# Two key chunks in one maximum: b + relu(a - b), with Relu on ScalarE, and a group's operands loaded in six transfers

## The chip, the cores and the metric

One core of a Trainium2 chip. The number to predict is the device time of the whole kernel in microseconds, the median over runs.

## What is computed

Two transformer layers on 2048 tokens of width 128, each with adaptive layer norms, causal attention of 16 heads of width 8, and a mixture of experts. The change lies in the attention alone. For each layer:

```python
scores = jnp.einsum('bhqd,bhkd->bhqk', q, k) / jnp.sqrt(jnp.float32(HEAD_DIM))
scores = jnp.where(causal, scores, -jnp.inf)
attn = jax.nn.softmax(scores, axis=-1)
out = jnp.einsum('bhqk,bhkd->bhqd', attn, v)
```

Layer one has one sequence of 2048 tokens, with projections and rotary positions ahead of this; layer two runs through the same attention code with its own q and k.

## The kernel before, in words

**Operands.** Every float32 value of q and k is split into three bf16 parts (hi, mid, lo), stored in DRAM (`q_parts`, `k_parts`) and loaded as the nine products of parts: 9 x 8 rows of `QS` and `KS`, for the 4 heads of a group. Rows 96 to 103 of `QS` take the softmax's shift, so that the matmul of scores subtracts the row maximum by itself. Heads go in 4 groups of 4 (`GH`); two groups have buffers at a time (`QS[g % 2]`).

**Units and steps.** A unit is a pair (group g, query chunk Q of 512 tokens); `UNITS` lists 16 in a written order, numbered from 0. Unit 2 is (0, 2), unit 4 is (0, 3), unit 6 is (1, 3), unit 9 is (2, 3), and unit 10 is (3, 3), the first of group 3. A step is one block of 128 keys of a unit, 160 in a layer: scores of the four heads in two halves (TensorE, L931, with the causal mask at L935), Exp of each half (ScalarE, L978), and the product with the values (TensorE, L949).

**Maxima first.** Before a unit can be scored, the maximum of each query's scores must be known. For each head j, block qb of 128 queries and key chunk c of 512, TensorE makes a tile of scores in one of three rotating PSUM buffers (`mxb`, L898), 640 tiles a layer, and VectorE takes its maximum: a plain reduction (L996) below the diagonal, a masked add and maximum (L998) on it. When a unit's last tile is done, VectorE joins the chunks (L1003) and splits the result in two bf16 numbers; TensorE turns them into rows ("turn", L904), VectorE copies them (L1012), and SyncE moves the rows into `QS` (L838). Only then do the unit's scores run.

**Order.** `schedule()` (L77 to L159) writes one list, `ORDER`, in which tiles, turns, scores, values, and the normalization and output of finished units ("norm", "attT", "out") are interleaved. It keeps a clock for TensorE, VectorE and ScalarE by built-in costs and takes a tile when its buffer would be free before the next scores could start. A turn comes `TURN_LAG` tiles after its unit's last one. TensorE runs through this list strictly in order; so a wait in it holds everything behind it.

**Loads.** Group 0's rows are loaded by SyncE in pieces during the projections. Groups 1 to 3 are loaded by GpSimd's queue in `load_group` (L753): 13 transfers, of which 3 are under way. Group 1's start after the first shift row is in (`shift_set[0]`, L861), those of groups 2 and 3 after the last step of the group whose buffers they take (L870). SyncE's queue also issues the expert weights behind the turns (L841).

```python
for n, (dst, src) in enumerate(moves):
    if n >= UNDER_WAY:
        eng.wait_ge(done[n % UNDER_WAY], 16 * (before * PER_SEM[n % UNDER_WAY] + n // UNDER_WAY))
    eng.dma_start(dst, src).then_inc(done[n % UNDER_WAY], 16)
```

## Time and profile before

| | |
|---|---|
| median of 3 runs | 1350.62 us (1349.40 to 1352.48) |
| span of the profiled execution | 1351.6 us |
| TensorE busy | 1152.9 us, 85% |
| VectorE busy | 962.7 us, 71% |
| ScalarE busy | 695.5 us, 51% |
| GpSimd busy | 240.5 us, 18% |
| maximum tiles on TensorE (L898) | 5120 matmuls, 1280 tiles |
| plain maxima (L996) | 768 instructions, 497.3 us |
| masked maxima (L998) | 512 instructions, 240.9 us |
| Exp (L978) | 640 instructions, 545.1 us |

The span and the runs agree within 0.1%, and the profiled execution has no time of its own in the results beside its span. Attention takes some 62 to 527 us in layer one and 685 to 1150 us in layer two. Busy times of TensorE are long where matmuls overlap in its pipeline, so they say less than the starts do.

### The profile page before, as it was taken

The page shows a single profiled execution, that of the slowest core. Times are in us where ns is not written, and L with a number is a line of the kernel's source. Part 1 is how long each engine was busy: PE and PEld are TensorE (multiplying, and loading weights), DVE is VectorE, ACT ScalarE, POOL GpSimd, SP SyncE. Part 2 cuts the span into 40 slices and gives each one's busy share as a digit, 9 for nine tenths or more (in the row PEclk, how much of TensorE's full clock was granted, in tenths as well). Part 3 has the DMA queues.
Part 4 walks back from the last instruction along what each step waited for, and adds up shares of the span by engine and source line. Part 5 has one row for each costly group of instructions (what it writes and reads, how often), then busy time and mean ns, then how long its engine had stood idle before and what let it go on. Part 6 is the DMA issues. An engine that isn't in the chain of part 4 may idle for free. (4 is left out here: it accounts for less than half of the span.)

```text
span 1351.6 us, 39302 instructions
## 1 busy us (share of the span) xinstructions
PE 1152.9 (85%) x16626; PEld 581.8 (43%) x16627; DVE 962.7 (71%) x2700; ACT 695.5 (51%) x929; POOL 240.5 (18%) x271
## 2 busy tenths in 40 slices
PE   5878999999899997297368899999899999778993
PEld 4423434434344444175123343444334454546662
DVE  5888989989698853511558998989788882564553
ACT  4424657666567674142334465766666668323330
POOL 2440000101000000277121000100200000135761
PEclk9678989999899997599678898999999999689997
DMA  4441000503200000221353111330400000011123
GB/s 142 142 80 41 19 19 19 92 19 55 57 3 5 5 3 2 45 54 53 95 154 65 35 37 36 67 65 4 76 3 4 5 4 3 1 40 38 48 47 107
DMA packets 38022, 60.46 MB, mean 45 GB/s; under 512 B 6288, under 2 KB 29104, under 8 KB 36720
## 3 DMA queue, kind: packets, MB, share of 16 engines
q0 software_dynamic: 7648, 24.47, 9.2%
q1 hardware_dynamic: 30208, 33.57, 8.6%
q8 instruction: 129, 2.11, 0.7%
q14 instruction: 37, 0.30, 0.1%
HBM read 42.84 MB, written 14.12 MB: 42 GB/s over the span
## 5 line engine op out<-in xcount | busy, mean ns | idle before, releaser
L978 ACT ACTIVATE probs_at<-st 128x1024 f32<-128x1024 f32 (+3 forms) x640 | 545.1, 897 | 323.2 <-PE st L931 221.1
L996 DVE TENSOR_REDUCE mxp_at<-mx 128x1 f32<-128x512 f32 x768 | 497.3, 685 | 69.1 <-PE mx L898 67.6
L898 PE MATMUL mx<-ks,qs 128*32 128x512 bf16 (+3 forms) x5120 | 390.8, 367 | 40.5 <-DVE mxp_at L996 11.4
L931 PE MATMUL st<-qs,ks 128*32 128x512 bf16 (+3 forms) x5120 | 363.5, 355 | 10.6 <-DMA qs<-shrow_at 8.1
L949 PE MATMUL av<-probs_at,vs 128*32 128x512 f32 (+3 forms) x2560 | 290.9, 530 | 0.3
L898 PEld LDWEIGHTS mx<-ks,qs 128*32 128x32 bf16 x5120 | 137.2, 97 | 344.3 <-DVE mxp_at L996 140.6
L998 DVE CUSTOM_DVE_ANT_0 junk_at<-mx,maskN 128x384 f32<-128x384 f32 (+3 forms) x512 | 240.9, 485 | 39.3 <-PE mx L898 36.2
L931 PEld LDWEIGHTS st<-qs,ks 128*32 128x32 bf16 x5120 | 133.9, 98 | 97.8 <-ACT probs_at L978 22.6
L1274 POOL DMA_INDIRECT taken<-table,token x71 | 68.1, 959 | 251.1 <-DVEq L1063 218.3
L935 PE MATMUL st<-maskTb,identb 128*32 128x128 bf16 x2048 | 103.8, 220 | 0.0
L949 PEld LDWEIGHTS av<-probs_at,vs 128*32 128x32 f32 x2560 | 69.7, 111 | 47.8 <-issue 5.6
L768 POOL DMA_DIRECT2D qs<-in_zrow_dram x6 | 3.6, 598 | 404.0 <-PE av L949 390.1
L935 PEld LDWEIGHTS st<-maskTb,identb 128*32 128x32 bf16 x2048 | 55.4, 98 | 16.9 <-issue 1.9
L1612 DVE TENSOR_TENSOR hid_f<-st,sg_f 128x352 f32<-128x352 f32 x39 | 20.5, 525 | 49.4 <-ACT sg_f L1585 49.4
L1280 POOL DMA_INDIRECT eo<-eo_f,dest x39 | 38.4, 985 | 25.8 <-DVE eo_f L1623 22.5
L998 DVE DVE_READ_ACCUMULATOR2_ANT mxp_at<- 128x1 f32 x512 | 42.5, 83 | 0.0
L1585 ACT ACTIVATE sg_f<-st 128x352 f32<-128x352 f32 x39 | 18.1, 464 | 47.4 <-PE st L1531 47.4
L768 POOL DMA_DIRECT2D qs<-q_parts x54 | 28.0, 521 | 70.7 <-DMA qs<-q_parts 50.4
L1530 PE MATMUL st<-weights,hTt_f 128*128 x78 | 33.1, 507 | 8.5 <-ACT hTt_f L1579 5.8
L1361 POOL TENSOR_TENSOR weights<-weights,gates 128x384 f32<-128x384 f32 x1 | 1.0, 987 | 187.1 <-POOLq L823 187.1
L1579 ACT ACTIVATE hTt_f<-mx,modc 128x128 f32<-128x128 f32 x39 | 17.8, 458 | 27.2 <-PE mx L1525 27.1
L1531 PE MATMUL st<-weights,hTt_f 128*128 x78 | 29.4, 459 | 0.0
(271 smaller groups left out, 1043.5 us busy)
## 6 DMA issues: line engine op xcount, KB each, us to landing
qs<-q_parts POOLq DMA_DIRECT2D x54, 128.0 KB, 5.7
ks<-k_parts POOLq DMA_DIRECT2D x18, 384.0 KB, 6.7
weights<-in_w_dram SPq DMA_DIRECT2D x16, 256.0 KB, 3.0
table<-rows SPq DMA_DIRECT2D x8, 260.0 KB, 5.4
got_pj<-eo SPq DMA_DIRECT2D x4, 512.0 KB, 5.5
got_cb<-eo SPq DMA_DIRECT2D x4, 512.0 KB, 5.4
weights<-in_dw_dram SPq DMA_DIRECT2D x3, 576.0 KB, 4.9
weights<-in_gw_dram SPq DMA_DIRECT2D x3, 528.0 KB, 3.8
```

Of the source, the lines that this page charges most:

```text
L768: eng.dma_start(dst, src).then_inc(done[n % UNDER_WAY], 16)
L898: mm = pe.matmul(buf[z:z + 32, 0:w], QS[p][:, j, (4 * Q + qb) * P + z:(4 * Q + qb) * P + z + 32], KS[p][:, j, c * CH:c * CH + w], start=Tr ...
L931: mm = pe.matmul(st[half][z:z + 32, y, off:CH], KS[p][:, j, kb * P + z:kb * P + z + 32], QS[p][:, j, Q * CH + off:(Q + 1) * CH], start=Tru ...
L935: mm = pe.matmul(st[half][z:z + 32, y, off:off + P], m.identb[:, z:z + 32], m.maskTb[:], start=False, stop=True, tile_position=(0, z), ski ...
L949: mm = pe.matmul(avb[32 * j:32 * j + 32, off:CH], VS[p][:, kb, j, :], probs[:, s % 2, j, off:CH], start=kb == 0, stop=kb == TPC * Q + 3, t ...
L978: act.activation(probs[:, s % 2, 2 * half:2 * half + 2, off:CH], st[half][:, :, off:CH], ACT.Exp, scale=SCALE).then_inc(exp_done[half], 1)
L996: ins = v.tensor_reduce(dst, buf[:, 0:w], AX.X, ALU.max)
L998: ins = v.tensor_tensor_reduce(junk[:, k % MXBUF, 0:w], buf[:, 0:w], m.maskN[:, CH - w:], 1.0, -3e38, ALU.add, ALU.max, dst)
L1274: g.indirect_dma_start(out=m.got[e][:, t4], out_offset=None, in_=dram[f"table{L}"], in_offset=bass.IndirectOffsetOnAxis(ap=m.token[:, n:n ...
L1280: g.indirect_dma_start(out=dram[f"eo{L}"], out_offset=bass.IndirectOffsetOnAxis(ap=m.dest[:, n:n + 1], axis=0), in_=rows, in_offset=None). ...
L1530: pe.matmul(G[z % 2][:, 0:FF1], hT[z % 2][:], gw[:, bass.ds(e, 1), :], start=True, stop=True)
L1531: pe.matmul(U[z % 2][:, 0:FF1], hT[z % 2][:], uw[:, bass.ds(e, 1), :], start=True, stop=True).then_inc(gu_ready, 1)
```

## The change

For units with Q of 2 or 3 the tile of key chunk 0 (a) and its reduction go. In its place TensorE makes a tile of the difference, q times (k0 - k1), a matmul with the same queries against a new operand `KD`; ScalarE writes relu of it to one of three SBUF buffers; and VectorE, when the tile of chunk 1 (b) is there, adds and takes the maximum in one two-input instruction: max(a, b) = b + relu(a - b). `KD` is made once per layer by GpSimd from the stored parts of k (nine instructions of 128x512, one behind the other), stored to DRAM, and loaded like k, with a copy per group buffer. SyncE waits for that store (`kd_stored`) before its first shift row. The planner's costs change, and it knows the new tiles; `UNITS`, the order of units, stays. The 13 transfers of a group become six that are issued without a wait between them: zero rows, k, three of q, and `KD`. Group 1's load waits for the shift of unit 1 (`shift_set[1]`).

```diff
 def max_tiles(g, Q):
-    return [(g, Q, j, qb, c) for qb in range(TPC) for j in range(GH) for c in range(Q + 1)]
+    return [(g, Q, j, qb, c) for qb in range(TPC) for j in range(GH) for c in range(Q >= 2, Q + 1)]
+
+
+def paired(m):
+    return m[1] >= 2 and m[4] == 1
 
 
...
+def max_order():
+
+    tiles = [m for g, Q in UNITS for m in max_tiles(g, Q)]
+    at = [i for i, m in enumerate(tiles) if paired(m)]
+    ahead = {}
+    for i in at:
+        ahead.setdefault(max(0, i - DIFF_LEAD), []).append(tiles[i])
+    out, due = [], []
+    for i, m in enumerate(tiles):
+        out += [("diff", x) for x in ahead.get(i, [])]
+        out.append(("max", m))
+        if due and due[0][0] <= i:
+            out.append(("turn", due.pop(0)[1]))
+        u = UNITS.index(m[:2])
+        if i + 1 == len(tiles) or UNITS.index(tiles[i + 1][:2]) != u:
+            due.append((i + TURN_LAG, u))
+    return out + [("turn", u) for _, u in due]
...
-LOADS = 1 + Q_LOADS + K_LOADS
-UNDER_WAY = 3
-PER_SEM = [len(range(z, LOADS, UNDER_WAY)) for z in range(UNDER_WAY)]
+LOADS = 1 + 1 + 3 + 1
...
-def load_group(eng, m, L, dram, g, done, before):
-
-
-    q, k = (dram[f"{n}_parts{L}"].tensor for n in "qk")
-    moves = [(m.QS[g % 2][SHIFT0:SHIFT0 + 2 * GH], bass.AP(dram["zrow"].tensor, 0, [[T, 2 * GH], [0, GH], [1, T]]))]
+def load_diff(eng, m, L, dram, g, done):
+
+    eng.dma_start(m.KD[g % 2][0:9 * HD].rearrange("p j t -> p (j t)"), bass.AP(
+        dram[f"kd_parts{L}"].tensor, g * GH * CH, [[0, 3], [H * CH, 3 * HD], [1, GH * CH]])).then_inc(done, 16)
+
+
+def load_group(eng, m, L, dram, g, done):
+
+    clear_shift(eng, m, dram, g % 2, done)
+    eng.dma_start(m.KS[g % 2][0:9 * HD].rearrange("p j t -> p (j t)"), bass.AP(
+        dram[f"k_parts{L}"].tensor, g * GH * T, [[0, 3], [H * T, 3 * HD], [1, GH * T]])).then_inc(done, 16)
     for a in range(3):
-        for b in range(3):
-            r = (3 * a + b) * HD
-            moves.append((m.QS[g % 2][r:r + HD], bass.AP(q, (a * P + g * GH) * T, [[H * T, HD], [T, GH], [1, T]])))
-    for a in range(3):
-        r = 3 * a * HD
-        moves.append((m.KS[g % 2][r:r + 3 * HD], bass.AP(k, g * GH * T, [[H * T, 3 * HD], [T, GH], [1, T]])))
-    for n, (dst, src) in enumerate(moves):
-        if n >= UNDER_WAY:
-            eng.wait_ge(done[n % UNDER_WAY], 16 * (before * PER_SEM[n % UNDER_WAY] + n // UNDER_WAY))
-        eng.dma_start(dst, src).then_inc(done[n % UNDER_WAY], 16)
+        eng.dma_start(m.QS[g % 2][3 * a * HD:3 * (a + 1) * HD].rearrange("p j t -> p (j t)"), bass.AP(
+            dram[f"q_parts{L}"].tensor, (a * P + g * GH) * T, [[0, 3], [H * T, HD], [1, GH * T]])).then_inc(done, 16)
+    load_diff(eng, m, L, dram, g, done)
...
                 loads = list(weight_loads)
+                sp.wait_ge(kd_stored, 16 * (L + 1))
                 for item in ORDER:
...
+                hi, mid, lo = (m.parts[1][:, a, :] for a in range(3))
+                d, t = (m.weights[:, KD_AT + i * CH:KD_AT + (i + 1) * CH] for i in range(2))
+                kd = m.weights[:, KD_AT + 2 * CH:KD_AT + 2 * CH + 3 * CH // 2].bitcast(BF).rearrange("p (a c) -> p a c", a=3)
+
+                def chained(ins):
+                    ins.then_inc(kd_chain.sem, 1)
+                    g.wait_ge(kd_chain.sem, kd_chain.next())
+
+                chained(g.tensor_tensor(d, hi[:, 0:CH], hi[:, CH:2 * CH], ALU.subtract))
+                chained(g.tensor_tensor(t, mid[:, 0:CH], mid[:, CH:2 * CH], ALU.subtract))
+                chained(g.tensor_tensor(d, d, t, ALU.add))
+                chained(g.tensor_tensor(t, lo[:, 0:CH], lo[:, CH:2 * CH], ALU.subtract))
+                chained(g.tensor_tensor(d, d, t, ALU.add))
+                chained(g.tensor_copy(kd[:, 0], d))
+                chained(g.tensor_tensor(t, d, kd[:, 0], ALU.subtract))
+                chained(g.tensor_copy(kd[:, 1], t))
+                chained(g.tensor_tensor(kd[:, 2], t, kd[:, 1], ALU.subtract))
+                g.dma_start(bass.AP(dram[f"kd_parts{L}"].tensor, 0, [[CH, P], [P * CH, 3], [1, CH]]), kd).then_inc(kd_stored, 16)
+                for p in range(2):
+                    g.memset(m.KD[p][64:P].bitcast(F32), 0.).then_inc(kd_set, 1)
+                g.wait_ge(kd_set, 2 * (L + 1))
+                g.wait_ge(kd_stored, 16 * (L + 1))
+                load_diff(g, m, L, dram, 0, kd_first)
                 if L == 0:
                     for z, rows in enumerate((KS[1], QS[1])):
                         g.memset(rows[64:P].bitcast(F32), 0.).then_inc(pool_set, 1)
                         g.wait_ge(pool_set, 5 + z)
                     g.dma_start(KS[1][SHIFT0:SHIFT0 + 2 * GH], dram["zo"]).then_inc(s_("ones_in1"), 16)
-                g.wait_ge(shift_set[0], 16 * (L * (NU // 4) + 1))
-                load_group(g, m, L, dram, 1, kq_loaded[1], loads_before(1))
+                g.wait_ge(shift_set[1], 16 * (L * (NU // 4) + 1))
+                load_group(g, m, L, dram, 1, kq_loaded[1])
...
-                    pe.wait_ge(mx_free, RB + k + 1)
-                    if kind == "max":
+                    if k >= MXBUF and ROT[k - MXBUF][0] == "diff":
+                        pe.wait_ge(diff_done, L * ND + DIFF_OF[ROT[k - MXBUF][1]] + 1)
+                    else:
+                        pe.wait_ge(mx_free, freed(k - MXBUF) if k >= MXBUF else MXBUF + L * NDVE)
+                    if kind in ("max", "diff"):
                         gg, Q, j, qb, c = x
...
+                        if kind == "diff" and k == DIFFS[0]:
+                            pe.wait_ge(kd_first, 16 * (L + 1))
+                        keys = m.KD[p][:, j, :] if kind == "diff" else KS[p][:, j, c * CH:c * CH + w]
                         for z in range(0, P, 32):
                             mm = pe.matmul(buf[z:z + 32, 0:w], QS[p][:, j, (4 * Q + qb) * P + z:(4 * Q + qb) * P + z + 32],
-                                           KS[p][:, j, c * CH:c * CH + w], start=True, stop=True, tile_position=(0, z), skip_group_check=True)
+                                           keys, start=True, stop=True, tile_position=(0, z), skip_group_check=True)
                         mm.then_inc(mx_ready, 1)
                     elif kind == "turn":
                         pe.wait_ge(shift_split, UB + x + 1)
...
-                for s, (g, Q, kb) in enumerate(STEPS):
-                    off = step_off(s)
-                    act.wait_ge(av_done, SB + s + 1)
-                    for half in range(2):
+                def rectify(k):
+                    n = DIFF_OF[ROT[k][1]]
+                    if n >= RELUS:
+                        act.wait_ge(mx_free, freed(ROT_OF[ROT[DIFFS[n - RELUS]][1]]))
+                    elif L:
+                        act.wait_ge(mx_free, MXBUF + NDVE)
+                    act.wait_ge(mx_ready, RB + k + 1)
+                    act.activation(relu[:, n % RELUS], mxb[k % MXBUF][:], ACT.Relu).then_inc(diff_done, 1)
+
+                for item in ORDER:
+                    if item[0] == "rot" and ROT[item[1]][0] == "diff":
+                        rectify(item[1])
+                    elif item[0] == "scores":
+                        _, s, half = item
+                        off = step_off(s)
+                        if half == 0:
+                            act.wait_ge(av_done, SB + s + 1)
                         act.wait_ge(st_ready[half], SB + s + 1)
                         act.activation(probs[:, s % 2, 2 * half:2 * half + 2, off:CH], st[half][:, :, off:CH], ACT.Exp,
                                        scale=SCALE).then_inc(exp_done[half], 1)
-                    if kb == 0 and s:
-                        evacuate(UNIT[s] - 1)
+                        if half == 1 and STEPS[s][2] == 0 and s:
+                            evacuate(UNIT[s] - 1)
                 evacuate(NU - 1)
...
                     v.sem_inc(mx_free, MXBUF)
                 for k, (kind, x) in enumerate(ROT):
+                    if kind == "diff":
+                        continue
                     buf = mxb[k % MXBUF]
                     v.wait_ge(mx_ready, RB + k + 1)
                     if kind == "max":
                         g, Q, j, qb, c = x
                         u, w = UNITS.index((g, Q)), max_width(x)
                         dst = mxp[:, u % 4, qb * GH + j, c:c + 1]
-                        if c < Q:
+                        if paired(x):
+                            n = DIFF_OF[x]
+                            v.wait_ge(diff_done, L * ND + n + 1)
+                            ins = v.tensor_tensor_reduce(relu[:, n % RELUS], buf[:], relu[:, n % RELUS], 1.0, -3e38, ALU.add, ALU.max, dst)
+                        elif c < Q:
                             ins = v.tensor_reduce(dst, buf[:, 0:w], AX.X, ALU.max)
                         else:
                             ins = v.tensor_tensor_reduce(junk[:, k % MXBUF, 0:w], buf[:, 0:w], m.maskN[:, CH - w:], 1.0, -3e38,
                                                          ALU.add, ALU.max, dst)
                         ins.then_inc(mx_free, 1)
                         if (j, qb, c) == (GH - 1, TPC - 1, Q):
-                            v.wait_ge(mx_free, RB + k + 1 + MXBUF)
-                            v.tensor_reduce(mx[:, u % 4, :], mxp[:, u % 4, :, 0:Q + 1], AX.X, ALU.max, negate=True).then_inc(max_final, 1)
+                            v.wait_ge(mx_free, freed(k))
+                            v.tensor_reduce(mx[:, u % 4, :], mxp[:, u % 4, :, Q >= 2:Q + 1], AX.X, ALU.max, negate=True).then_inc(max_final, 1)
```

Here `NDVE` counts the rotating tiles that VectorE frees and `freed(k)` those up to tile k; `DIFF_OF` numbers the difference tiles.

Three places of the new order, each as it was and as it is.

SyncE at the start of layer one's attention (`stored1`, `stored2` say that the parts of k are in DRAM; `shrow_at` is the row of shifts):

```order
L748 DMA ks<-k_parts 24x4x512 [waits stored1]
L748 DMA ks<-k_parts 24x4x512 x2
L748 DMA ks<-k_parts 24x4x1024 [waits stored2]
L748 DMA ks<-k_parts 24x4x1024 x2
L838 DMA qs<-shrow_at 8x4x512 [waits shift_row] x3
L842 DMA weights<-in_w_dram 128x512 x2
```

```order
L794 DMA ks<-k_parts 24x4x512 [waits stored1]
L794 DMA ks<-k_parts 24x4x512 x2
L794 DMA ks<-k_parts 24x4x1024 [waits stored2]
L794 DMA ks<-k_parts 24x4x1024 x2
L892 DMA qs<-shrow_at 8x4x512 [waits shift_row,kd_stored]
L892 DMA qs<-shrow_at 8x4x512 [waits shift_row] x2
L896 DMA weights<-in_w_dram 128x512 x2
L892 DMA qs<-shrow_at 8x4x512 [waits shift_row]
```

The first shift row has a second condition, `kd_stored`, and all later ones stand behind it.

TensorE around the turn of unit 2 in layer one: the last steps of unit 1, then tiles, the turn (`nsh_at`), and tiles up to the scores of unit 2. In the count of a row four matmuls are one tile:

```order
L931 MATMUL st<-qs,ks 32x128 x4
L935 MATMUL st<-maskTb,identb 32x128 x4
L949 MATMUL av<-probs_at,vs 32x256 x4
L898 MATMUL mx<-ks,qs 32x512 x36
L898 MATMUL mx<-ks,qs 32x128 x4
L898 MATMUL mx<-ks,qs 32x512 x4
L904 MATMUL mx<-identb,nsh_at 8x128 x4
L898 MATMUL mx<-ks,qs 32x128 x4
L898 MATMUL mx<-ks,qs 32x512 x4
L898 MATMUL mx<-ks,qs 32x128 x4
L898 MATMUL mx<-ks,qs 32x512 x4
L898 MATMUL mx<-ks,qs 32x128 x4
```

```order
L1019 MATMUL st<-qs,ks 32x128 x4
L1023 MATMUL st<-maskTb,identb 32x128 x4
L1037 MATMUL av<-probs_at,vs 32x256 x4
L986 MATMUL mx<-ks,qs 32x512 x4
L986 MATMUL mx<-ks,qs 32x128 x4
L986 MATMUL mx<-ks,qs 32x512 x4
L992 MATMUL mx<-identb,nsh_at 8x128 x4
L986 MATMUL mx<-ks,qs 32x128 x4
L986 MATMUL mx<-ks,qs 32x512 x4
L986 MATMUL mx<-ks,qs 32x128 x4
L986 MATMUL mx<-ks,qs 32x512 x4
L986 MATMUL mx<-ks,qs 32x128 x4
```

Between the last values of unit 1 and the turn stood 11 tiles; now 3 do, and all of unit 2's other tiles stand ahead of that.

ScalarE at the start of unit 6's scores in layer one (the copy moves the finished sums of unit 5):

```order
L978 ACTIVATE probs_at<-st 128x2x128 [waits st_ready1]
L978 ACTIVATE probs_at<-st 128x1024 [waits st_ready0,av_done]
L978 ACTIVATE probs_at<-st 128x1024 [waits st_ready1]
L971 COPY avs_at<-av 128x512 [waits mx_ready,av_done]
L978 ACTIVATE probs_at<-st 128x1024 [waits st_ready0,av_done]
L978 ACTIVATE probs_at<-st 128x1024 [waits st_ready1]
L978 ACTIVATE probs_at<-st 128x1024 [waits st_ready0,av_done]
```

```order
L1068 ACTIVATE relu_at<-mx 128x512 [waits mx_ready,mx_free]
L1079 ACTIVATE probs_at<-st 128x1024 [waits st_ready0,av_done]
L1068 ACTIVATE relu_at<-mx 128x512 [waits mx_ready,mx_free]
L1079 ACTIVATE probs_at<-st 128x1024 [waits st_ready1]
L1059 COPY avs_at<-av 128x512 [waits mx_ready,av_done]
L1068 ACTIVATE relu_at<-mx 128x512 [waits mx_ready,mx_free]
L1079 ACTIVATE probs_at<-st 128x1024 [waits st_ready0,av_done]
L1079 ACTIVATE probs_at<-st 128x1024 [waits st_ready1]
L1068 ACTIVATE relu_at<-mx 128x512 [waits mx_ready,mx_free]
L1079 ACTIVATE probs_at<-st 128x1024 [waits st_ready0,av_done]
L1079 ACTIVATE probs_at<-st 128x1024 [waits st_ready1]
```

Relus stand between Exps, some between the two halves of one step.

## Rows read from the trace of the kernel before

**Rows 1.** Busy time by stretch: us, then each engine's (instructions), clock, DMA share, GB/s
```profile
62.00:77.50 15.50, 9.89 (x116) 3.29 (x120) 14.83 (x50) 0.00 (x0) 8.41 (x5) 0.61 0.49 129
...
191.00:344.00 153.00, 150.75 (x2688) 65.21 (x2684) 135.58 (x340) 105.75 (x123) 14.73 (x28) 0.99 0.25 49
...
354.00:495.00 141.00, 139.08 (x2604) 63.87 (x2604) 118.84 (x345) 96.49 (x118) 0.00 (x0) 0.99 0.03 7
```

**Rows 2.** Timeline of ScalarE, layer one: start, us, what, [idle before, releaser]
```profile
98.85 1.02 ACT L978 ACTIVATE probs_at<-st 128x1024 f32<-128x1024 f32 x1 [10.94 <-PE st L931]
...
131.17 2.16 ACT L978 ACTIVATE probs_at<-st 128x1024 f32<-128x1024 f32 x2 [12.40 <-PE st L931]
...
192.13 1.02 ACT L978 ACTIVATE probs_at<-st 128x1024 f32<-128x1024 f32 x1 [10.60 <-PE st L931]
...
356.12 1.94 ACT L978 ACTIVATE probs_at<-st 128x1024 f32<-128x1024 f32 x2 [11.03 <-PE st L931]
```

**Rows 3.** Load of group 3: timeline of GpSimd and TensorE; DMA issues, KB, us to landing
```profile
319.54 0.58 POOL L768 DMA_DIRECT2D qs<-in_zrow_dram  x1 [61.79 <-PE av L949]
...
349.11 0.83 PE L898 MATMUL mx<-ks,qs 128*32 128x512 bf16 x12 [4.12 <-DMA ks<-k_parts]
...
qs<-q_parts POOLq DMA_DIRECT2D x54, 128.0 KB, 5.7
ks<-k_parts POOLq DMA_DIRECT2D x18, 384.0 KB, 6.7
```

**Rows 4.** Timeline of TensorE in a long stretch
```profile
404.81 1.03 PE L949 MATMUL av<-probs_at,vs 128*32 128x512 f32 x8
...
405.67 0.77 PE L898 MATMUL mx<-ks,qs 128*32 128x384 bf16 x12
...
406.26 0.60 PE L931 MATMUL st<-qs,ks 128*32 128x512 bf16 x8
...
406.69 0.39 PE L898 MATMUL mx<-ks,qs 128*32 128x512 bf16 x4
```

**Rows 5.** Groups by line and shape, TensorE, 361 to 495 us: busy, mean ns
```profile
L931 PE MATMUL st<-qs,ks 128*32 128x512 bf16 x588 | 44.9, 379 | 0.0
...
L898 PE MATMUL mx<-ks,qs 128*32 128x512 bf16 x488 | 40.7, 381 | 0.5 <-DVE mxp_at L998 0.2
...
L949 PE MATMUL av<-probs_at,vs 128*32 128x512 f32 x296 | 38.2, 592 | 0.0
```

**Rows 6.** Timeline and groups of VectorE and ScalarE, 131 to 344 us
```profile
241.35 1.88 DVE L996 TENSOR_REDUCE mxp_at<-mx 128x1 f32<-128x512 f32 x3
...
L998 DVE CUSTOM_DVE_ANT_0 junk_at<-mx,maskN 128x512 f32<-128x512 f32 x28 | 19.0, 687 | 3.1 <-PE mx L898 3.1
...
L971 ACT COPY avs_at<-av 128x512 f32<-128x512 f32 x7 | 4.1, 585 | 0.0
```

**Rows 7.** The starts of both attentions: timelines; GpSimd's groups; DMA issues
```profile
68.42 0.61 POOL L850 COPY vs<-vall 128x512 f32<-128x512 f32 x1 [9.99 <-DMA k_parts<-weights]
...
74.59 52.78 SPq L838 DMA_DIRECT2D qs<-shrow_at  x3
...
77.53 0.65 PE L931 MATMUL st<-qs,ks 128*32 128x512 bf16 x4
...
691.49 0.61 POOL L850 COPY vs<-vall 128x512 f32<-128x512 f32 x1 [5.53 <-DMA k_parts<-weights]
...
705.09 0.62 PE L931 MATMUL st<-qs,ks 128*32 128x512 bf16 x4 [3.96 <-DMA qs<-shrow_at]
...
L503 POOL TENSOR_TENSOR weights<-res,weights 128x512 bf16<-128x512 f32 x8 | 9.9, 1246 | 7.2 <-ACT weights L348 7.2
...
L220 POOL TENSOR_TENSOR qf<-tmp 128x512 f32<-128x512 f32 x4 | 6.2, 1552 | 25.3 <-DVE tmp L400 25.3
...
k_parts<-weights SPq DMA_DIRECT2D x4, 384.0 KB, 3.7
```

**Rows 8.** Waits, 150 to 500 us: waiting, releaser, us in total, times, longest
```profile
PEld st L931 <- ACT probs_at L978: 3.4, 10, 0.6
```

126 lines of the change are left out of this document (80 added, 46 removed).

## The prediction

> **What bounds the kernel now.** First the busy table by stretches of the first layer's attention [rows 1]. It shows two kinds of stretch. In the long ones (191 to 344, 354 to 495 us, and 131 to 181 like them) TensorE is busy 150.8 of 153 and 139.1 of 141 us, VectorE 89% and 84%, ScalarE 69% and 68%. In short ones like 344 to 354 us ScalarE is all but idle: no unit of scores is ready.
>
> The timeline of ScalarE gives these holes their length [rows 2]: it waits for scores 10.94, 12.40, 10.60 and 11.03 us, at the starts of units 1, 2, 4 and 9. Layer two repeats all four. The first three are VectorE's: a unit can't be scored before all its maxima are taken. The fourth is not: TensorE waits 4.12 us for keys of the next group [rows 3], and the turn of unit 9 stands three tiles behind that wait.
>
> Is a "busy" TensorE full? Its matmul ends are modelled, so I go by starts [rows 4]: from 406.26 to 406.69 eight score matmuls take 0.43 us, eight value matmuls 0.86 (404.81 to 405.67), three maximum tiles 0.59 (405.67 to 406.26), so a 512-wide one about 0.21. With these, the counts of 361 to 495 us [rows 5] make: 588 wide score matmuls 31.6 us, 488 of maxima 26, 296 of values 31.6; masks, narrow forms and transposes, in proportion to their width, about 33. That is 122 us of work in 134. The other 12 us, 9%, are gaps, most of them ahead of maximum tiles whose buffer VectorE still holds. So TensorE bounds the long stretches with VectorE close behind, and what VectorE gives up there is worth only TensorE's small gaps.
>
> **The change, part by part.** (a) Units with Q of 2 or 3 give up one reduction per head and block: 8 units x 16 = 128 a layer. One costs VectorE 0.60 us: three in a row take 1.88, of which the last 0.68 [rows 6]. The pass that stays becomes the two-input form. The masked pass, which also reads PSUM and SBUF, takes 687 ns at this width, as long as a reduction, so the exchange adds nothing. VectorE loses 128 x 0.60 = 77 us a layer. TensorE's tiles stay 640 a layer, since each pair has a difference tile in place of chunk 0's. ScalarE gains 128 Relus. Nearest row: the copy of the same width from PSUM, mean 585 ns [rows 6]. Two Exps of 1.02 us take 1.94 together [rows 2], so some 0.10 overlap and a Relu costs 0.48: 61 us a layer. 64 of them fall into 191 to 344 us, where ScalarE goes from 105.8 to 137 of 153 us, with little slack.
>
> (b) **The long stretches**, 344 us a layer. A share of 9% would be 31 us. Turns, transposes and some scores hold part of it, and a difference tile will now wait for ScalarE, behind Exps of 1.02 us. I take 9 us a layer as gained, between 0 and 31: -18.
>
> (c) **The hole before unit 2.** Before, 11 tiles stand between the last scores of unit 1 and the turn of unit 2; now 3 do (order rows of TensorE). Eight at 0.60 us are 4.8, less 0.8 for what was packed ahead of it, part of that into the hole before unit 1, which is otherwise the same: -4 a layer, -8. Behind the turn stand 10 tiles where 9 did, and its row's way through VectorE, SyncE and the DMA stays. The hole before unit 4 has 9 tiles ahead of its turn before and after, and 11 instead of 7 behind it: I put it at 0, between -3 and +2.
>
> (d) **The load of a group.** Thirteen transfers, three under way, run from 319.54 to 349.11 us, 29.6 us [rows 3]; keys come last. Six issue at once, in some 3 us. The 384 KB pieces land in 6.7 us with three under way, 176 GB/s; the 128 KB ones in 5.7, 69 GB/s. The new load carries 2.8 MB (zero rows, q, k, and 0.3 for the difference): 16 us at the first rate, 20 with issue and landing. It is there at 340, before TensorE asks at 345, and the 10 us hole shrinks to 7 tiles and the turn's way, 3.2 us: -7 a layer, -14. At the old length it gives nothing. Group 1 now waits for the shift of unit 1 instead of unit 0: its load would run from 107 to 127 us, just before TensorE wants it at about 128 (the end of unit 1's scores, 118.5, plus the delay of (e)). What is late there is lost; I price it at 0.
>
> (e) **The start.** This is the cost. GpSimd now does 9 steps of 128x512 behind the copy that ends at 69.03 us, and SyncE holds the first shift row until their store has landed. Seven subtractions or additions at 1.2 us (the 1246 ns row) and two casts at 0.9 (between that and the copy's 0.61), with handshakes 0.5: 10.7 us. The store is like the 384 KB one: 3.7, plus issue 0.5. So the row leaves at 83.9 instead of 74.59, and with the 2.94 us that it takes until TensorE starts at 77.53, the first scores come at 86.9: +9.3 [rows 7]. In layer two the copy ends at 692.10, so they come at 709.9 instead of 705.09: +4.8. Nothing hides it: TensorE stands in front of the first scores, VectorE starves behind it, and unit 1's maxima shift too. The granted clock at the start is 0.61 [rows 1], the lower of two levels for much of it, and a longer idle time should keep it low: +2 for both. Together +16. Bounds: 9 steps at 0.61 and at 1.55 us (GpSimd's slowest two-input row) give +4 and +28. The zeroing of the second buffers, 3.5 us each, comes behind all this, but before group 1's load asks for GpSimd.
>
> Sum: +16 - 18 - 8 + 0 - 14 = **-24 us** against the profiled span of 1351.6: 1327.6. The median of the runs is 1.0 lower: **1327**.
>
> A rule speaks against (a): the Trainium skill, ScalarE: Activation LUTs, Rules for kernel authors, sends relu to VectorE, and budgets about 0.3 us plus 0.83 ns an element for an ACTIVATE. By that estimate a Relu is 0.73 us, ScalarE would be busy 152 of the 153 us, term (b) would be gone and the sum would give 1345. The copy's row has 0.585 before any overlap, so the sum goes by the row.
>
> **Rivals.** *ScalarE's queue becomes the wait* (slower). ScalarE works in order: a Relu often stands behind an Exp of 1.02 us, and until it is done one of only three rotating buffers is held; the Exps behind it move back by 0.48 us and the next scores with them. For it: ScalarE at 89%, and Relus between the two Exps of a step in the new order. Against: tiles and scores are interleaved anew with the Relus in their place, and scores hardly wait for Exps now, 3.4 us in 350 [rows 8]. If one Relu in four costs TensorE half an Exp, 64 x 0.51 = 33 us, (b) turns from -18 to +33 and the sum is +27: 1378. It decides from +6 in (b), 0.02 us lost per Relu.
>
> *The loads gain nothing and the start costs nearly its upper bound* (no change). Six transfers share the same DMA engines; if the small pieces' 69 GB/s is what they get, (d) is 0 and the sum is -10; with the start at +26 it is 0: 1351.
>
> *VectorE was the pace after all* (faster still). If three quarters of the 9% go, (b) is -46 and the sum -52: 1299. Against: it needs a ScalarE that is never late.
>
> That the change doesn't do what it says can be excluded for the maxima, whose instructions the order shows; for the load it is the second rival.
>
> **Chances.** Forecast (1303 to 1347) 0.56; the larger gain 0.12; no change 0.07; slower, by ScalarE's queue or by a start at its upper bound with late loads, 0.25. A measurement of this kernel tells 0.2% (2.7 us) from no change: faster 0.68, same 0.07, slower 0.25. The range, **1302 to 1361**, leaves out about 1 in 10 on each side and holds the bounds of (e) with those of (d), and half the way to the first rival.
>
> **What would show it.** VectorE's busy time falls by about 150 us and ScalarE's rises by 120 to 150. The idle time before unit 2 falls from 12.4 to about 8 us, that before unit 9 from 11 to about 4. The first scores come at 87 us, in layer two 5 us later than before by the end of its projections. In the long stretches gaps ahead of maximum tiles become rare, and new waits for a Relu stay at a few us. Wrong would be: ScalarE over 90% busy there with TensorE waiting for it, keys that still arrive 25 us after their trigger, or first scores later than 92 us.

## The result and the profile after

The changed kernel takes **1401.57 us** (median of 4 runs, 1399.91 to 1403.02) where the kernel before, run beside it, took 1351.55: a ratio of 1.0363, 95% interval 1.0330 to 1.0395. It is slower by 50 us; the forecast was 24 us faster, and its range ended at 1361. The profiled execution has a span of 1398.1 us, 46.5 more than before.

Busy times first, from the page's first and fifth part (busy time, mean ns, idle time before it and what ended it):

```profile
PE 1162.2 (83%) x16626; PEld 589.6 (42%) x16627; DVE 817.3 (58%) x2700; ACT 827.2 (59%) x1185; POOL 247.1 (18%) x255
...
L1079 ACT ACTIVATE probs_at<-st 128x1024 f32<-128x1024 f32 (+3 forms) x640 | 557.5, 900 | 147.3 <-PE st L1019 78.7
...
L1105 DVE CUSTOM_DVE_ANT_0 junk_at<-mx,maskN 128x384 f32<-128x384 f32 (+3 forms) x512 | 241.6, 485 | 72.9 <-PE mx L986 69.8
L1101 DVE CUSTOM_DVE_ANT_0 relu_at<-mx,relu_at 128x512 f32<-128x512 f32 x256 | 176.9, 691 | 181.3 <-PE mx L986 178.9
...
L1068 ACT ACTIVATE relu_at<-mx 128x512 f32<-128x512 f32 x256 | 154.1, 602 | 82.1 <-PE mx L986 77.8
L1103 DVE TENSOR_REDUCE mxp_at<-mx 128x1 f32<-128x512 f32 x256 | 175.9, 687 | 28.9 <-PE mx L986 28.6
...
L986 PE MATMUL mx<-kd_at,qs 128*32 128x512 bf16 x1024 | 107.5, 398 | 32.4 <-DMA kd_at<-kd_parts 29.1
```

VectorE gives up 145 us and ScalarE takes on 132, as intended. What is new stands in the last row: TensorE waits 29.1 us for the differences' keys, which did not exist before. An order that puts other work there could have hidden them.

The three stretches of [rows 1], at their new places (columns as there):

```profile
62.00:82.40 20.40, 9.35 (x96) 2.74 (x92) 12.73 (x47) 0.00 (x0) 14.95 (x15) 0.58 0.31 90
206.00:354.00 148.00, 139.55 (x2386) 59.29 (x2381) 92.84 (x307) 121.07 (x164) 8.14 (x14) 0.98 0.25 49
380.00:518.00 138.00, 136.08 (x2552) 61.63 (x2552) 98.98 (x335) 109.16 (x145) 0.00 (x0) 1.00 0.02 4
```

VectorE falls from 89% to 63% of the second stretch, and it was to be TensorE's gain; but TensorE is busy 139.6 of 148 us there where it was busy 150.8 of 153. ScalarE is at 82% there; 89% was forecast.

Where are the 46.5 us? ScalarE copies the value sums once at each unit's start. Those copies date the units in both traces (start of the copy, us):

| unit | 1 | 4 | 5 | 6 | 9 | 12 | 13 | end of 15 |
|---|---|---|---|---|---|---|---|---|
| before, layer one | 101.1 | 194.4 | 235.5 | 267.0 | 357.9 | 461.2 | 480.7 | 520.1 |
| after | 107.1 | 200.9 | 244.6 | 285.8 | 380.7 | 481.6 | 504.3 | 543.4 |
| before, layer two | 729.7 | 822.4 | 863.5 | 895.7 | 984.9 | 1089.6 | 1109.0 | 1148.4 |
| after | 757.2 | 851.2 | 895.0 | 937.4 | 1033.1 | 1134.0 | 1156.7 | 1195.8 |

The loss by stretch is 6.0 up to unit 1, then 17.3 in the attention of layer one (436.3 against 419.0 us), 4.2 up to unit 1 of layer two, 19.9 in its attention (438.6 against 418.7), and 0.9 gained behind it: 46.5. In both layers nearly all of it falls between units 4 and 6 (12.3 and 12.9), between 6 and 9 (3.8 and 6.6) and between 12 and 13 (3.3 in both). From unit 9 to 12, the longest stretch without a load, the new kernel is faster, by 2.4 and 3.8 us. The 4.2 us are less sure than the rest: among the versions below that share one start, the time from the end of one attention to unit 1 of the next goes from 208.5 to 214.5 us.

The load of group 2, as [rows 3] had that of group 3, in the timeline of GpSimd and TensorE:

```profile
243.95 0.57 POOL L774 DMA_DIRECT2D qs<-in_zrow_dram  x1 [135.78 <-PE av L1037]
244.51 0.63 POOL L808 DMA_DIRECT2D ks<-k_parts  x1
...
246.95 0.62 POOL L801 DMA_DIRECT2D kd_at<-kd_parts  x1
...
259.80 0.61 PE L1019 MATMUL st<-qs,ks 128*32 128x512 bf16 x2 [3.50 <-issue]
...
273.78 0.62 PE L986 MATMUL mx<-kd_at,qs 128*32 128x512 bf16 x4 [2.66 <-DMA kd_at<-kd_parts]
```

The DMA issues of the page, with the KB of one and the us from issue to landing:

```profile
ks<-k_parts POOLq DMA_DIRECT2D x6, 1152.0 KB, 3.9
qs<-q_parts POOLq DMA_DIRECT2D x18, 384.0 KB, 16.1
...
kd_at<-kd_parts POOLq DMA_DIRECT2D x8, 288.0 KB, 24.9
```

All six are issued within 3.6 us, yet TensorE can go on only 29.8 us after the trigger. Group 3's load takes 27.2: triggered at 339.20, used at 366.42.

The landing times of the first two rows can't be taken singly. All six transfers add to one semaphore, and the profile tells a landing by its count. Between 243.9 and 248.5 us, when the keys' 1152 KB would have landed, the load's queue moved 0.40 MB in all (packets, MB, share of 16 engines' time):

```profile
q0 software_dynamic: 635, 0.40, 52.2%
```

Near its end the load is thin. Only a fifth of the DMA engines' time is taken, at 83 GB/s (columns as in [rows 1]):

```profile
263.00:268.00 5.00, 5.00 (x94) 2.44 (x90) 3.12 (x17) 3.73 (x4) 0.00 (x0) 0.99 0.21 83
```

Group 3's wait, and the hole before unit 2, are what ScalarE's timeline still shows of [rows 2]:

```profile
136.52 2.01 ACT L1079 ACTIVATE probs_at<-st 128x1024 f32<-128x1024 f32 x2 [10.32 <-PE st L1019]
...
367.15 0.60 ACT L1068 ACTIVATE relu_at<-mx 128x512 f32<-128x512 f32 x1 [9.53 <-PE mx L986]
```

The start, answering to [rows 7]:

```profile
65.37 0.61 POOL L904 COPY vs<-vall 128x512 f32<-128x512 f32 x1 [8.47 <-DMA k_parts<-weights]
66.06 1.16 POOL L919 TENSOR_TENSOR weights<-weights 128x512 f32<-128x512 bf16 x1
...
74.37 0.61 POOL L926 CAST weights<-weights 128x512 bf16<-128x512 f32 x1
75.06 1.15 POOL L927 TENSOR_TENSOR weights<-weights 128x512 bf16<-128x512 f32 x1
...
79.71 0.85 SPq L892 DMA_DIRECT2D qs<-shrow_at  x1
...
82.41 0.62 PE L1019 MATMUL st<-qs,ks 128*32 128x512 bf16 x4 [8.27 <-DMA qs<-shrow_at]
```

And the waits of 150 to 500 us, answering to [rows 8], which had 3.4 us for Exps (waiting, releaser, us in total, times, longest). First two rows of the kernel before, then the changed kernel:

```profile
PEld mx L898 <- DVE mxp_at L996: 54.1, 165, 0.7
PEld mx L898 <- DVE mxp_at L998: 34.0, 117, 0.5
```

```profile
PEld mx L986 <- DVE mxp_at L1105: 26.5, 91, 0.5
PEld mx L986 <- DVE mxp_at L1101: 25.3, 65, 1.2
...
PEld mx L986 <- ACT relu_at L1068: 14.9, 42, 0.7
PEld mx L986 <- DVE mxp_at L1103: 13.5, 42, 0.8
...
PEld st L1019 <- ACT probs_at L1079: 11.0, 27, 0.8
```

The weight loads of maximum tiles waited 88.1 us for VectorE before and wait 65.3 now. But 14.9 us for Relus are new, and the waits for Exps have grown from 3.4 to 11.0: most of what VectorE gives up is waited for elsewhere. These waits partly overlap with matmuls that still run, so they aren't lost time one for one.

### The profile page after: what moved, and what is told of

Its sections match the earlier page's. It is cut to its first block and busy times, and to the rows that moved or that the text cites. A ratio compares the mean times of both kernels' runs of the same rounds, so it can differ in the third digit from the quotient of the medians.

```text
span 1398.1 us, 40050 instructions
## 1 busy us (share of the span) xinstructions
PE 1162.2 (83%) x16626; PEld 589.6 (42%) x16627; DVE 817.3 (58%) x2700; ACT 827.2 (59%) x1185; POOL 247.1 (18%) x255
## 5 line engine op out<-in xcount | busy, mean ns | idle before, releaser
L1079 ACT ACTIVATE probs_at<-st 128x1024 f32<-128x1024 f32 (+3 forms) x640 | 557.5, 900 | 147.3 <-PE st L1019 78.7
L986 PE MATMUL mx<-ks,qs 128*32 128x512 bf16 (+3 forms) x4096 | 325.0, 361 | 35.3 <-DVE mxp_at L1101 9.0
L1037 PE MATMUL av<-probs_at,vs 128*32 128x512 f32 (+3 forms) x2560 | 295.4, 535 | 0.3
L1101 DVE CUSTOM_DVE_ANT_0 relu_at<-mx,relu_at 128x512 f32<-128x512 f32 x256 | 176.9, 691 | 181.3 <-PE mx L986 178.9
L986 PEld LDWEIGHTS mx<-ks,qs 128*32 128x32 bf16 x4096 | 113.7, 98 | 271.4 <-DVE mxp_at L1105 73.8
L1068 ACT ACTIVATE relu_at<-mx 128x512 f32<-128x512 f32 x256 | 154.1, 602 | 82.1 <-PE mx L986 77.8
L1103 DVE TENSOR_REDUCE mxp_at<-mx 128x1 f32<-128x512 f32 x256 | 175.9, 687 | 28.9 <-PE mx L986 28.6
L986 PE MATMUL mx<-kd_at,qs 128*32 128x512 bf16 x1024 | 107.5, 398 | 32.4 <-DMA kd_at<-kd_parts 29.1
L986 PEld LDWEIGHTS mx<-kd_at,qs 128*32 128x32 bf16 x1024 | 29.2, 96 | 86.8 <-issue 38.6
L1637 PE MATMUL st<-weights,hTt_f 128*128 x78 | 33.0, 505 | 8.8 <-ACT hTt_f L1686 5.9
```

The lines of the kernel that those rows point to most:

```text
L986: mm = pe.matmul(buf[z:z + 32, 0:w], QS[p][:, j, (4 * Q + qb) * P + z:(4 * Q + qb) * P + z + 32], keys, start=True, stop=True, tile_positi ...
L1037: mm = pe.matmul(avb[32 * j:32 * j + 32, off:CH], VS[p][:, kb, j, :], probs[:, s % 2, j, off:CH], start=kb == 0, stop=kb == TPC * Q + 3, t ...
L1068: act.activation(relu[:, n % RELUS], mxb[k % MXBUF][:], ACT.Relu).then_inc(diff_done, 1)
L1079: act.activation(probs[:, s % 2, 2 * half:2 * half + 2, off:CH], st[half][:, :, off:CH], ACT.Exp, scale=SCALE).then_inc(exp_done[half], 1)
L1101: ins = v.tensor_tensor_reduce(relu[:, n % RELUS], buf[:], relu[:, n % RELUS], 1.0, -3e38, ALU.add, ALU.max, dst)
L1103: ins = v.tensor_reduce(dst, buf[:, 0:w], AX.X, ALU.max)
```

## The experiments

Five causes were on the table: the length and order of the group loads, the time at which the order asks for them, the start, ScalarE's queue, and the planner's other numbers. Ratios are to the kernel before, with 95% intervals. The kernel before was run anew beside each group of experiments, with medians of 1353.3 to 1356.0 us; so between groups ratios tell more than microseconds.

**The five transfers alone**, in the kernel before (no difference, no pairing, old order):

```diff
-LOADS = 1 + Q_LOADS + K_LOADS
-UNDER_WAY = 3
-PER_SEM = [len(range(z, LOADS, UNDER_WAY)) for z in range(UNDER_WAY)]
+LOADS = 1 + 1 + 3
...
-    for n, (dst, src) in enumerate(moves):
-        if n >= UNDER_WAY:
-            eng.wait_ge(done[n % UNDER_WAY], 16 * (before * PER_SEM[n % UNDER_WAY] + n // UNDER_WAY))
-        eng.dma_start(dst, src).then_inc(done[n % UNDER_WAY], 16)
```

> The kernel before with its loads of groups 1 to 3 in five transfers issued without waits (zero rows, k, three of q); everything else as before, no difference operand. Theory A (the unthrottled load is the fault: it fills the DMA engines, is no quicker in all, and delays TensorE's instruction fetch): the keys arrive about 24 to 28 us after the trigger instead of 29, waits of 2 to 4 us with no releaser appear on TensorE during the loads, three to five of them, and the time is 1350 to 1360. Theory B (Relus in ScalarE's queue are the fault and the loads are fine): the waits of 4.1 and 2.5 us for keys go with the holes around them, no new waits, 1335 to 1343. I expect A: 1353.

1355.98 us, ratio 1.0015 (0.9990 to 1.0040): no change. The wait for keys at group 3 is gone (unit 9's copy at 355.6 instead of 357.9), but group 1's load now runs beside the turn and shift row of unit 1: TensorE stands 6.03 us at 89.77 us, in the middle of a run of mask matmuls and with no releaser, 15.8 us behind that load's trigger, and in layer two it waits 5.15 us for unit 1's row instead of 1.88. Three to five such stalls were expected; there is one. The transfers as such neither give nor take in sum.

**The start.** SyncE's wait for the differences' store goes from ahead of the first shift row to ahead of the first expert weights.

```diff
-                sp.wait_ge(kd_stored, 16 * (L + 1))
                 for item in ORDER:
...
+                            if u == 2:
+                                sp.wait_ge(kd_stored, 16 * (L + 1))
```

> The changed kernel with SyncE's wait for the store of the difference moved from ahead of the first shift row to ahead of the first expert weights, whose region it protects. The first scores should come about 5 us earlier in layer one and 3 to 4 in layer two (the row then waits for VectorE alone). Theory C (the start is lost one for one, since TensorE stands behind it): 1392 to 1394 against 1401.6. Theory D (the start is hidden by a later wait, for the difference operand of group 1 or for its load): no change within 2 us. I expect C: 1393.

1393.77 us, ratio 1.0303 (1.0257 to 1.0350): 8 us of the 50. The copy of unit 1 comes at 97.6 us instead of 107.1; the attentions are 3.3 us longer and 0.9 shorter (439.6 and 437.7). The start's cost was the wait, not GpSimd's work.

**Fourteen transfers, three under way**, in the changed kernel (an excerpt; pieces of 8 and 24 rows as before, the difference's keys second):

```diff
+        if n >= UNDER_WAY:
+            eng.wait_ge(done[n % UNDER_WAY], 16 * (before * PER_SEM[n % UNDER_WAY] + n // UNDER_WAY))
```

> The changed kernel with its loads of groups 1 to 3 as before: pieces of 8 and 24 rows, three under way, the difference operand as one more transfer, the second of 14. Same order of tiles as the changed kernel. Theory A: the 12 us of waits without a releaser vanish, but the load takes 29 to 31 us, so that the 31 us of waits at the first tiles of groups 2 and 3 stay or grow by a few us, since the order asks for them early: 1390 to 1402. Theory B: nothing changes but the loads' own length: 1400 to 1410.

1435.56 us, ratio 1.0612 (1.0563 to 1.0660), 34 us slower still, and above what was expected. Three waits of TensorE in layer one alone:

```profile
135.76 1.15 PE L998 MATMUL mx<-ks,qs 128*32 128x512 bf16 x12 [11.63 <-DMA ks<-k_parts]
...
287.53 0.62 PE L998 MATMUL mx<-kd_at,qs 128*32 128x512 bf16 x4 [14.27 <-DMA ks<-k_parts]
...
388.56 0.62 PE L998 MATMUL mx<-kd_at,qs 128*32 128x512 bf16 x4 [16.85 <-DMA ks<-k_parts]
```

With this order every group is waited for: the six first tiles of groups wait 85.9 us in all, where they waited 34.3 with six transfers at once. Groups 2 and 3 of layer one take 36.1 and 34.6 us from trigger to first tile instead of 29.8 and 27.2. So the same bytes come sooner as six transfers. The 34 us are less than the 51.6 us of added waits: some of those waits took the place of others. TensorE's stalls without a releaser in mid-stream (3.50, 3.17 and 1.80 us in the changed kernel) are gone here, as the expectation had it; the kernel before has none either.

**Unpaired, all else kept** (`paired` returns False, chunk 0 gets its tile again):

> The changed kernel with the maxima as before: no difference tiles, no Relu, plain reductions for chunks 0 and 1; the difference operand is still made, stored and loaded, and the planner keeps the new costs, with its order made for these tiles. It tells what the pairing itself is worth beside loads and start. Theory B: the Relus cost some 30 us, so this gains: 1365 to 1375. Theory A: the pairing gives nothing and costs nothing in the long stretches but makes the order ask for groups 2 and 3 earlier (9 steps after the trigger instead of 13), so part of the waits for loads goes: 1378 to 1390. Theory E (the pairing gains what was forecast in the holes and long stretches, 10 to 20 us a layer, and other things hide it): 1405 to 1425.

1378.73 us, ratio 1.0185 (1.0143 to 1.0227): 23 us less. Taking the pairing out of this kernel gains. And no keys are waited for at groups 2 and 3: with unpaired tiles the planner asks for group 2 in step 60, with paired ones in step 56. Stalls without a releaser remain, of 2.34, 2.22 and 4.16 us, each 18 to 19 us behind the trigger of a load.

**The planner's numbers alone**: the unpaired version without any difference (no steps on GpSimd, no store, five transfers):

> The changed kernel with no difference of keys at all: unpaired maxima, five transfers a group, nothing computed or waited for at the start, group 1 asked after unit 0's shift as before. What is left of the change is the planner's new costs, and thereby the order of the units, beside the five transfers at once (which alone made 1356.0). Theory A (the order and the loads cost the rest): the unpaired version with the difference kept took 1378.7; less 8 for the start, 1368 to 1373. Rival (the numbers of the planner are harmless, and the unpaired version lost its time by the start and by the difference's own transfers): 1353 to 1360.

1358.06 us, ratio 1.0020 (0.9997 to 1.0044). The new costs do no harm without pairing (attention of layer one 415.4 us, before 419.0). The 1368 to 1373 that my theory gave was a miss; the rival's range held it. Against the unpaired version with the difference, the attentions are 8.3 and 9.0 us shorter. Beside the start, it differs by the difference's own transfer and by asking for group 1 a unit earlier, so the transfer of 288 KB may cost much of that; it wasn't taken apart.

**The load reckoned at 28 us** in the changed kernel:

```diff
-LOAD_US = 18.
+LOAD_US = 28.
```

> The changed kernel with one number of its planner raised: a group's load is reckoned 28 us instead of 18, so the order takes the first tile of group 2 in step 60 instead of 56 and that of group 3 in step 91 instead of 88; the transfers are the same. Theory A (the waits for the difference's keys, 30.8 us in four places, are lost outright): 1401.6 - 20 to 30 = 1372 to 1382. Theory B (VectorE and ScalarE fall behind elsewhere, the wait for keys only takes the place of another): 1392 to 1402.

1380.94 us, ratio 1.0212 (1.0173 to 1.0252): 21 us for one number. The waits for the differences' keys shrink from 30.8 us to 1.7, 1.2 and 2.9, all in layer two. A stall without a releaser stays, in the middle of eight score matmuls, 15.6 us behind a trigger. First TensorE's timeline, then the instruction queue's packets of 226 to 241 us, of 242 to 257.5 and of 258 to 260.2 (there none is listed):

```profile
260.14 0.39 PE L1019 MATMUL st<-qs,ks 128*32 128x512 bf16 x2 [3.23 <-issue]
```

```profile
q8 instruction: 3, 0.05, 1.4%
...
q8 instruction: 1, 0.02, 0.6%
```

From 226 to 241 us, ahead of the trigger at 244.57, three packets of instructions came in; in the 15.5 us with the load, one. That fits a TensorE that has run out of instructions while the queues are full. Such stalls stand in the versions with five or six transfers at once and in none with three under way; that it is the instructions wasn't tested apart, so it stays a reading.

**The same, with the difference asked for early and the store's wait late.** The difference of a group goes out when the last difference tile two groups back is done, on its own semaphore; that of group 1 goes out at the start (an excerpt):

```diff
+                    g.wait_ge(diff_done, L * ND + LAST_DIFF[gg - 2] + 1)
+                    load_diff(g, m, L, dram, gg, kd_in[gg % 2])
                     g.wait_ge(av_done, 2 + SB + LAST[gg - 2] + 1)
```

> As with the planner's 28, and the difference's keys of a group asked for as soon as the last difference tile two groups back is done, on a semaphore of their own, so that five transfers are left for the trigger; and SyncE's wait for the store of the difference moved from ahead of the first shift row to ahead of the first expert weights. Theory A with the start: 8 less than the version with 28 alone for the start and 2 to 6 less for the shorter load: 1360 to 1372. Theory B (ScalarE's queue costs it): no lower than 1385.

1365.53 us, ratio 1.0079 (1.0046 to 1.0112). 8 of the 15 us are the start, by the run above. Layer one's attention is down from 424.8 to 419.4 us; layer two's is up from 426.2 to 430.2. There the early difference of group 3 falls into group 2's load, 11 us behind the trigger, and TensorE waits at the first tile of group 2, which waits for that load:

```profile
866.53 0.56 POOL L776 DMA_DIRECT2D qs<-in_zrow_dram  x1 [55.73 <-PE av L1045]
...
877.45 0.62 POOL L803 DMA_DIRECT2D kd_at<-kd_parts  x1 [7.48 <-ACT relu_at L1076]
...
899.20 0.62 PE L994 MATMUL mx<-kd_at,qs 128*32 128x512 bf16 x4 [5.74 <-issue]
```

**The planner's old costs** in the changed kernel (handshakes, pace, Exp, row's way, 26 us for a load; the Relu's cost kept):

```diff
-CLOCK = 2330.
-LOAD_US = 18.
+CLOCK = 2400.
+LOAD_US = 26.
-    to_dve = to_act = .23
-    back = .13
+    to_dve = to_act = .2
+    back = .1
-            act = max(act, pe + to_act, av_end.get(s - 2, 0) + back) + .07 + 2 * w * .000833
+            act = max(act, pe + to_act) + .19 + 2 * w * .000833
```

(also 45 us instead of 55 for group 1, 2.4 instead of 2.8 for the row, 0.003 a matmul instead of 0.012)

> The changed kernel, pairing, six transfers and start kept, with the planner's costs and latencies put back to those of the kernel before (load 26 us, shorter handshakes, Exp with 0.19 fixed), the Relu's cost kept. The first tile of group 2 comes in step 58, that of group 3 in step 90. Theory A: the waits for keys fall by half or more, 1380 to 1390. Rival (the new numbers describe the chip better and the old ones would make a worse order): 1400 or more.

1372.10 us, ratio 1.0135 (1.0104 to 1.0166), 29 us less with start and loads as in the change, and less than either theory gave.

**q asked for only when the keys have landed**, on the 1365.5 version:

```diff
+    eng.wait_ge(done, 16 * (LOADS * before + 2))
     for a in range(3):
```

> The version with the plan at 28, the difference's keys early and the store's wait late (1365.5), with one thing more: GpSimd waits until the zero rows and the keys of a group have landed before it asks for the three transfers of q, so 1.2 and then 1.2 MB are under way instead of 2.4. Theory A2 (a full set of DMA queues holds back TensorE's instruction fetch: waits of 5.7 and 2.8 us with no releaser in layer two): those waits shrink and the time is 3 to 8 us lower, 1357 to 1362. Rival (the load only gets longer, as with three small transfers under way): 1368 or more, with new waits for q.

1398.73 us, ratio 1.0330 (1.0297 to 1.0364), 33 us slower. The rival was right. First TensorE at the first tiles of groups 1 and 2, then what this run alone shows of the load: the landings, the keys now apart from q, and a window in which all but one packet are the keys' (columns as in [rows 1]):

```profile
127.52 1.15 PE L995 MATMUL mx<-ks,qs 128*32 128x512 bf16 x12 [10.36 <-issue]
...
276.64 0.62 PE L995 MATMUL mx<-kd_at,qs 128*32 128x512 bf16 x4 [7.94 <-issue]
```

```profile
ks<-k_parts POOLq DMA_DIRECT2D x6, 1152.0 KB, 17.7
qs<-q_parts POOLq DMA_DIRECT2D x18, 384.0 KB, 9.6
```

```profile
247.00:259.00 12.00, 12.00 (x192) 4.57 (x184) 9.08 (x30) 10.48 (x13) 0.00 (x0) 1.00 0.20 83
```

The keys alone take 17.7 us, not 3.9, and leave four fifths of the DMA engines' time unused: 83 GB/s at a share of 0.20, the pace of the end of the load in the changed kernel. Three of 16 engines would be a share of 0.19, and the source of the keys starts with a dimension of three copies (`[[0, 3], ...]` in `load_group`), as do those of q and of the difference. Whether another form of these transfers would be faster wasn't tried. With q held back behind the keys, the two can't overlap, and group 2's load takes 34.9 us, though the difference's keys aren't in it.

The two waits of TensorE shown above are at first tiles of a group, where it waits for the load. So "issue" at a group's first tile is the load, and I had read the 5.74 us above wrongly as instructions when I wrote this expectation. The stall in mid-group at 260.14 is another thing.

**A shorter Relu**, 64 of 512 columns, in the 1365.5 version (it leaves out part of the maximum; the other columns hold a constant, and VectorE writes its sum elsewhere):

```diff
-                    act.activation(relu[:, n % RELUS], mxb[k % MXBUF][:], ACT.Relu)
+                    act.activation(relu[:, n % RELUS, 0:64], mxb[k % MXBUF][:, 0:64], ACT.Relu)
```

> The 1365.5 version with a Relu over 64 of the 512 columns; the other columns of its output hold a constant, and VectorE still adds and reduces 512, so the maximum that is subtracted is too large (it leaves out part of the maximum and its output is not the reference's). VectorE's second operand no longer overwrites the Relu's buffer. Theory B (ScalarE's queue: Relus hold back Exps and tiles): a Relu costs some 0.25 us less, 32 us a layer off ScalarE, and half to all of the 4 us a layer that pairing costs against the unpaired order, and of the 9 that it should have brought, comes: 1340 to 1357. Rival (TensorE is full and nothing that the other two engines give up is worth anything): 1361 to 1367.

1355.54 us, ratio 0.9997 (0.9974 to 1.0019), 10 us less, in theory B's range. A Relu takes 227 ns instead of 602 (groups of 150 to 500 us):

```profile
L1077 ACT ACTIVATE relu_at<-mx 128x64 f32<-128x64 f32 x108 | 24.5, 227 | 28.7 <-PE mx L995 25.1 <-DVE mxp_at L1116 2.9
```

96 us off ScalarE's work (256 x 0.375) give 10. But of these, 1.8 and 7.8 us come from the two attentions, most of the latter at group 3 of layer two; the long stretches give under 1 us each.

**Old costs, early difference, late store wait** together:

> The 1365.5 version with the old costs in the planner (as the 1372 version has them). That one lost 8 us at the start and some 2 us by loads; both are mended here: 1360 to 1364. Theory A says that the two mends add up, 1360; if the order is what the early keys make useless, 1365 to 1368.

**1347.62 us, ratio 0.9936 (0.9913 to 0.9960)**: 0.6% faster than the kernel before, clear of noise, and 12 us below the expectation. The early difference of group 3 now goes out 18.6 us behind the trigger:

```profile
855.47 0.56 POOL L776 DMA_DIRECT2D qs<-in_zrow_dram  x1 [52.44 <-PE av L1045]
...
874.07 0.62 POOL L803 DMA_DIRECT2D kd_at<-kd_parts  x1 [15.15 <-ACT relu_at L1076]
```

and at a group's first tile TensorE waits 1.0 us at most (group 1 of layer two). The attentions take 415.3 and 414.4 us.

**The unpaired version with group 1's load behind unit 1's row** (new costs, no difference):

```diff
-                g.wait_ge(shift_set[0], 16 * (L * (NU // 4) + 1))
+                g.wait_ge(shift_set[1], 16 * (L * (NU // 4) + 1))
```

> The unpaired order with the new planner costs and five transfers at once (1358.1), with group 1's load asked for after the shift row of unit 1 instead of unit 0. There TensorE waited 4.96 us for instructions at 91.2 and 4.18 us for the row of unit 1 at 733.0, both beside that load; without them 1348 to 1352, the first version below the kernel before. Rival (group 1's load is then late by what the row gains): 1355 to 1360.

1352.19 us, ratio 0.9992 (0.9958 to 1.0026): by the medians 6 us less than with the load ahead of the row, by the ratios 4, with intervals that overlap. The copy of unit 1 comes at 98.1 instead of 105.1 us.

**Which of the old numbers?** Four runs on the 1365.5 version. The Exp's cost alone:

> The 1365.5 version (plan at 28, early difference, late store wait, new planner costs) with the Exp's old cost alone (0.19 us fixed instead of 0.07, and not tied to the values two steps back). If it is this number that made the order with pairing 18 us slower than the old costs do (1347.6), 1348 to 1356; if it is the handshakes, 1362 to 1370.

1372.56 us, ratio 1.0109 (1.0074 to 1.0145), above both expectations. The handshakes and the pace alone:

> The 1365.5 version with the old handshakes and TensorE pace alone (0.20 and 0.10 us instead of 0.23 and 0.13, 0.003 a matmul instead of 0.012, 2.4 GHz instead of 2.33). The counterpart of the run with the old Exp cost: 1348 to 1356 if the handshakes were it, 1362 to 1370 if the Exp's cost was.

1369.99 us, 1.0096 (1.0065 to 1.0128). The row's way and group 1's time:

> The 1365.5 version with the two old numbers that neither of the last two runs put back: the turn row's way 2.4 us instead of 2.8 and group 1's load in at 45 instead of 55. If these carry the 18 us, 1347 to 1354; if the old costs only work together, 1363 to 1372.

1366.38 us, 1.0082 (1.0048 to 1.0116). And the first two together:

> The complement: old Exp cost and old handshakes together, the row's way 2.8, group 1 at 55 and the load at 28 as in the 1365.5 version. Its first tile of group 2 comes in step 58 and its tiles before the trigger of group 3 are 394, both as in the 1347.6 version. If the two work together (each alone gave nothing), 1347 to 1354; if not, 1363 to 1372.

**1349.33 us**, ratio 0.9989 (0.9967 to 1.0012). Each alone gives nothing, the two together 16 us by the medians and 12 by the ratios. The 1347.6 version's interval ends below this one's, so some of its gain, 2 us by the medians and 7 by the ratios, may lie in the other numbers. The order shows a difference at two places. Ahead of unit 5's first scores, where group 2's load is triggered, it puts 281 tiles in the changed kernel and in the 1365.5 version, 283 with either old cost alone, 268 with both, and 265 in the kernel before. Ahead of unit 8's, where group 3's is triggered, it puts 421, 404, 404 to 413, 392 and 397. Tiles ahead of a unit's scores move its steps back, and with them the trigger.

**The price of pairing.** The kernel before, with five transfers and the row first:

> The kernel before with five transfers at once (1356.0) and group 1's load behind the shift row of unit 1: unpaired, old costs. Beside the 1347.6 of the paired version with old costs it gives the price of pairing by itself. Theory P (pairing with the order right is a gain of a few us, and the row first gives the other): 1350 to 1353. Rival (the whole gain of the 1347.6 version is the load and the row, pairing gives nothing): 1346 to 1349.

1352.63 us, ratio 0.9974 (0.9946 to 1.0002). The paired version in the good order has 0.9936. Pairing is worth some 5 us, 0.4%, with intervals that overlap, and the two versions differ in small things besides: some costs of the planner, such as that of a unit's last maximum, stay new in the paired one, and the difference is made and loaded; in the profiles the attentions are 1.1 and 2.7 us shorter (415.3 and 414.4 against 416.4 and 417.1). The gain lies between units 1 and 4 (90.9 and 91.5 us against 94.2 and 94.4). In the long stretch from unit 9 to 12 the paired version is the slower one, 104.1 and 104.2 us against 103.2 and 103.1.

**The short Relu in the good order:**

> The 1347.6 version (pairing, old costs, early difference, late store wait) with a Relu over 64 of 512 columns and a constant in the others, so that it leaves out part of the maximum. Theory B (every Relu costs through ScalarE's queue, in any order): 1336 to 1342, as the same cut gave 10 us in the other order. Rival (the old order has room for the Relus): 1345 to 1349.

1347.00 us, ratio 0.9941 (0.9905 to 0.9978), no difference from 1347.62 (0.9936). The intervals leave room for some 5 us either way, and the profiled execution's attentions are 2.5 and 3.3 us shorter, so a cost of a few us isn't excluded.

## Why the prediction was wrong

**(a) held.** VectorE -145 us against -150 to -154, ScalarE +132 against 120 to 150. The two-input pass takes 691 ns, the masked one took 687. A Relu takes 602 ns by itself, and the start of the next Exp follows 0.49 us behind (107.61 and 108.10 us): my 0.48. The Trainium skill's budget (ScalarE: Activation LUTs, Rules for kernel authors), stated for a bias that comes as a pointer and an estimate of 0.73 us here, was too high. The slower time is not mainly the Relu's doing: shortening it gives nothing that can be measured in the good order.

**(b) failed: it took VectorE's release for TensorE's gain.** "TensorE's small gaps" seemed to give 2.4 and 3.8 us between units 9 and 12 (100.9 us). But the unpaired version with the same new costs takes 101.8 us there, so pairing gives 0.9 of that and the new order the rest. With the old costs pairing loses some 1 us in that stretch, and from unit 4 to 9 it loses 0.9 in layer one and gains 1.2 in layer two. Between units 12 and 13, 3 us were lost again, 22.7 us instead of 19.5, by the order: with both old costs it is 19.0. So of the 18 us forecast for the long stretches no run shows more than 1 or 2. The 9% of gaps were read rightly, but TensorE waits there for a buffer whichever engine frees it: its waits for VectorE fell from 88.1 to 65.3 us in 150 to 500 us, and 14.9 for Relus and 7.6 more for Exps stand in their place.

**(c) a small gain was there.** The idle time before unit 2 went from 12.40 to 10.32 us, not to 8. From unit 1 to unit 4 nothing came of it in this order (93.3 us before, 93.7 after). In the good order that stretch is 3.3 and 2.9 us shorter with pairing than without, near the 4 a layer of the forecast; that is more than pairing gives in all.

**(d) was the step that failed worst**, twice. It had 7 us gained a layer; between units 4 and 9, where the loads of groups 2 and 3 lie, 16.2 and 19.4 us were lost. First the size: I took the load at 176 GB/s, the rate of three 384 KB transfers under way, and got 20 us; it takes 27 to 30. The keys, which stand nearly first in the new load, take 17.7 us by themselves, at 83 GB/s. "At the old length it gives nothing" stood in the text, and the load came at about that length. Second, and larger, the overlap, which I let stand as it was: the order is planned around the load. The planner is told 18 us, and with paired tiles it asks for group 2 in step 56 (before: 61), 9 steps behind its trigger instead of 14. With unpaired tiles the same 18 us gave step 60 and did no harm, so it takes both: a load reckoned too short, and cheaper maxima that let the plan run ahead. A load about as long as before is then late by 30.8 us in five places. Raising the number gave 21 us back; asking early for the difference gave some 7, by subtraction. I had looked at where the order puts the turns and never at how many steps lie between a load's trigger and its first tile.

**(e) was half right.** First scores came at 82.41 us, not 86.9: GpSimd's nine steps take 10.2 us as reckoned, but behind a copy that ends at 65.98 in this execution instead of 69.03. In layer two unit 1 lost 4.2 more, by the forecast 4.8. In all 10 us by the copies, where I had 16, and 8 us are had by moving one wait. In layer one the cost itself was nearer than that: with the wait moved, unit 1 comes 9.5 us earlier (97.63 instead of 107.15), and asking for group 1 a unit later hides some of it, for it brings unit 1 forward by 6 us in the unpaired kernel (103.13 to 97.17). The upper bound of +28 doesn't follow from its row: nine steps at 1.55 us add 3.8 us a layer to the 16, which makes 24.

**The rivals.** "ScalarE's queue" named a time near the one that came, but not its cause: shortening the Relu gives 10 us in the 1365.5 order and nothing measurable in the good one. "The loads gain nothing" was the nearest, and stopped at zero, since I let the order stand still.

Of the 50 us, then, by the medians and in the order in which they were taken out: 8 are the start, 21 the load's number in the planner, 7 the difference's place in the load, 18 the planner's other costs, most of it only where the Exp's and the handshakes' stand together. That makes 54, down to 1347.6. The shares hang on that order: with the old costs put back first, all of them give 29, and the start and the difference's place 24 together.

What stays open: why the new costs, which alone do no harm unpaired, do harm with pairing. The counts show more tiles ahead of units 5 and 8; that these very tiles cost the 16 us wasn't tried apart. The size of pairing's gain isn't settled beyond some us, nor the cause of the stall at 260.14 us, nor what sets the length of a load.

## What to carry to other kernels

Where an order is planned around a duration, a change to that duration must be measured before the order is built on it: 18 us written down for a load that takes 27 to 30 cost 21 us with the new tiles, and no harm showed with the old ones; pairing at its best brought some 5. Read how many steps lie between a transfer's trigger and its first use, in both orders. And put a wait where its result is first needed: the store wait ahead of the first shift row cost 8 us and guarded nothing that the row touches.

## What the runs showed of the hardware

The same 2.8 MB came sooner as six transfers at once than as fourteen with three under way: 27.2 and 29.8 us from trigger to first tile against 34.6 and 36.1. The thirteen of the kernel before, without the 0.3 MB of the difference, took 29.6 [rows 3]. The keys' 1152 KB alone took 17.7 us at a fifth of the DMA engines' time, and the end of the six-transfer load of group 2 ran at the same 83 GB/s and 0.21. Splitting the load with a wait behind the keys made it 34.9 us long and the kernel 33 us slower.

A small transfer pays for what is under way when it is issued. The difference's 288 KB, on a semaphore of their own, took 21.8 us from issue to landing when issued 10.9 us into a group's load (the 1365.5 version) and 7.5 us when issued 18.6 us behind the trigger (the 1347.6 version).

Landings of transfers that add to one semaphore can't be told apart: the page gives 3.9 us for the keys, and they took 17.7 when nothing else was counted with them but the zero rows.

With five or six large transfers issued at once, TensorE stood 2.2 to 6.0 us with no releaser in several places, 15.6 to 18.7 us behind a trigger (3.50, 3.23, 6.03, 2.34, 2.22 and 4.16 us). With three under way no such stall of over 1.2 us is in either attention.
